# A graph kernel on one core: messages of the later passes in an array of their own, with the two groups of a chunk side by side

## The reference

```python
# layer 0: one pass, weighted
agg = segment_sum(adj_vals[:, None] * xw[edge_src], edge_dst)
# layer 1: messages gated by an MLP of the edge attributes, back to the source
msg = gate * h[dst] * (cw * mj)[:, None]
agg = segment_sum(msg, src);  tot = segment_sum(mj, src)
# layer 2: two weighted passes
x = segment_sum(x[src] * edge_weight[:, None], dst)
# layer 3 (Chebyshev, K = 4): three unweighted passes
prop = segment_sum(w[:, None] * h[row], col)
```

## Time and profile before

| | |
|---|---|
| time of three runs | 16256.79 us median, 16254.69 to 16295.25 |
| the profiled execution's own time | 16257.53 us, for a span of 16255.7 us |
| busy: PE, DVE, ACT, POOL | 10843.7, 12042.7, 7461.2, 7855.1 us |
| DMA queues: SP's, POOL's | 3065.78 MB, 57.2% of the 16 engines; 1034.11 MB, 16.5% |
| HBM read, written | 2932.16 MB, 1702.21 MB |

### The profile page before, as it was taken

How to read it: one execution, slowest core, us unless ns; L and a number is a source line. 1 busy time by engine, 2 the same in 40 slices (tenths; PEclk the granted TensorE clock), 3 DMA queues, 4 the chain that set the end, 5 groups by cost and what they waited for, 6 DMA issues and landing times. The chain is left out here.

```text
span 16255.7 us, 582040 instructions
## 1 busy us (share of the span) xinstructions
PE 10843.7 (67%) x194032; PEld 8861.6 (55%) x194033; DVE 12042.7 (74%) x25807; ACT 7461.2 (46%) x21291; POOL 7855.1 (48%) x7665
## 2 busy tenths in 40 slices
PE   5676666666610488867776677777776686676678
PEld 4555555555500366644555556666655565565556
DVE  9666666666633378789996788789778778777776
ACT  0121212121122267744445656766664475475466
POOL 0677777777777366013331067037307605713730
PEclk8777777777755599988888888999997797798789
DMA  8343333333467499879998798889779898988987
GB/s 339 111 124 124 123 123 123 123 123 123 123 170 179 114 364 350 291 257 341 331 309 246 241 337 324 280 307 353 274 261 375 319 313 332 373 277 309 384 289 238
DMA packets 1719990, 4103.19 MB, mean 252 GB/s; under 512 B 337506, under 2 KB 626240, under 8 KB 1719094
## 3 DMA queue, kind: packets, MB, share of 16 engines
q1 hardware_dynamic: 1288470, 3065.78, 57.2%
q0 software_dynamic: 431248, 1034.11, 16.5%
q10 hardware_dynamic: 144, 1.60, 0.0%
HBM read 2932.16 MB, written 1702.21 MB: 285 GB/s over the span
## 5 line engine op out<-in xcount | busy, mean ns | idle before, releaser
L1443 POOL DMA_INDIRECT messages<-exp_stage,exp_block_rows x3324 | 3555.9, 1070 | 4461.9 <-ACT exp_stage L1423 1830.6
L845 POOL DMA_INDIRECT records<-rec,row_i x3125 | 3113.0, 996 | 1444.6 <-issue 814.5
L1584 PEld LDWEIGHTS sum_sums<-sum_slots,sum_onehot 128*128 128x128 bf16 x93072 | 2521.5, 96 | 1135.8 <-issue 1133.7
L1584 PE MATMUL sum_sums<-sum_slots,sum_onehot 128*128 128x48 bf16 (+1 forms) x93072 | 2677.8, 183 | 625.6 <-DVE h L1510 485.3
L1541 ACT ACTIVATE sum_onehot<-iota_b,sum_late_places 128x128 bf16<-128x128 bf16 x5817 | 1910.1, 391 | 765.1 <-PE sum_sums L1584 681.0
L1301 PE MATMUL exp_rows<-tab,h 128*128 x39888 | 1811.7, 197 | 512.7 <-DVE h L1342 225.2
L1307 PE MATMUL exp_rows<-tab,h 128*128 x13296 | 1428.4, 282 | 932.1 <-ACT exp_stage L1423 688.0
L1301 PEld LDWEIGHTS exp_rows<-tab,h 128*128 128x128 bf16 x39888 | 1567.7, 102 | 872.5 <-issue 726.5
L1307 PEld LDWEIGHTS exp_rows<-tab,h 128*128 128x128 bf16 x13296 | 1208.5, 125 | 1151.8 <-issue 1118.9
L668 ACT COPY rec<-emeta 128x40 f32 (+1 forms) x625 | 140.2, 224 | 3064.3 <-DMA records<-rec,row_i 3064.3
L1342 DVE TENSOR_SCALAR h<-exp_places,pcol 128x2048 bf16<-128x2048 bf16 x1662 | 1298.9, 782 | 164.4 <-DMA exp_places<-src_places 140.7
(11 more groups left out here) (299 smaller groups left out, 22128.4 us busy)
## 6 DMA issues: line engine op xcount, KB each, us to landing
sum_slots<-messages SPq DMA_DIRECT2D x1662, 576.0 KB, 5.3
exp_places<-src_places SPq DMA_DIRECT2D x1662, 512.0 KB
sum_slots<-messages SPq DMA_DIRECT2D x277, 600.0 KB, 5.4
messages<-zeros SPq DMA_DIRECT2D x124, 1149.0 KB
l_places<-dst_places SPq DMA_DIRECT2D x277, 512.0 KB, 6.3
recc<-records SPq DMA_DIRECT2D x277, 448.0 KB, 4.7
l_gate<-records SPq DMA_DIRECT2D x277, 448.0 KB
records<-fill SPq DMA_DIRECT2D x215, 576.0 KB, 12.9
```

Source lines behind the costliest of these rows:

```text
L845: pool.indirect_dma_start(rec_dram, bass.IndirectOffsetOnAxis(ap=row_i[:, g, k:k + 1], axis=0), rec[:, g, k, :], None).then_inc(put[g], 16)
L1443: pool.indirect_dma_start(lines, bass.IndirectOffsetOnAxis(ap=row_d[:, c, g:g + 1], axis=0), stage[:, c, g, :], None, element_offset=0 if ...
L1584: last = pe.matmul(sums[:, c % RS, g, 0:width], onehot[:, c % RS, g * B + k, :], of[:, n * width:(n + 1) * width], start=n == 0, stop=n == ...
```

## The change

The array is split in two. `first_messages` has lines of 832 words: type values and the first pass's terms. `messages` holds nothing but terms, for the way back at rows of 600 words and for the later passes, over the same memory, at rows of 576. In both arrays the two groups of a chunk alternate: block p of the chunk's first group is row 2p of the chunk, block p of the second row 2p + 1. So `idx_d` and `idx` have to be turned into the new numbers, ten more instructions on DVE, and a chunk's load of partition p becomes one run of 4608 bytes (4800 on the way back). In the first pass the two runs of 2304 bytes stay two, 1024 bytes apart. The type loads of the gate stage stay two runs of 1024 bytes. Both arrays are set to zero.

```diff
-    LINE = ceil_div(UROW + ROW1 // 2, 32) * 32
+    LINE = UROW + ROW // 2
+    TERMS = ROW1 // 2
...
-    line_dram = nc.dram_tensor("messages", [NBLK, LINE], F32).ap()
-    terms_dram = line_dram.bitcast(BF16)[:, 2 * UROW:2 * UROW + ROW1]
-    msg_dram, back_dram = terms_dram[:, 0:ROW], terms_dram
+    line_dram = nc.dram_tensor("first_messages", [NBLK, LINE], F32).ap()
+    later_dram = nc.dram_tensor("messages", [NBLK * TERMS], F32).ap()
+    msg_dram = later_dram.bitcast(BF16)[0:NBLK * ROW].rearrange("(n f) -> n f", f=ROW)
+    back_dram = later_dram.bitcast(BF16).rearrange("(n f) -> n f", f=ROW1)
+
+    def in_pairs(rows):
+        return rows.rearrange("(c p g) f -> p c (g f)", p=P, g=CH)
...
+                    def zeros(k, i, first):
+                        if first:
+                            to, _, begin = zeroed[k]
+                            sp.dma_start(to[:, 0:begin], zero_dram[:, 0:begin]).then_inc(s_zero, 16)
+                            sp.dma_start(*pieces(k, 0, 1, R5 - 1)).then_inc(s_zero, 16)
+                        else:
+                            sp.dma_start(*pieces(k, i, 0, R5)).then_inc(s_zero, 16)
+
                     def turn(i, first, last):
                         windows_of(i, first, 1)
-                        if first:
-                            sp.dma_start(zeroed[:, 0:BEGIN], zero_dram[:, 0:BEGIN]).then_inc(s_zero, 16)
-                            sp.dma_start(*pieces(0, 1, 2)).then_inc(s_zero, 16)
-                        else:
-                            sp.dma_start(*pieces(i, 0, 3)).then_inc(s_zero, 16)
+                        zeros(0, i, first)
                         attrs(i, first, 1)
                         if not last:
                             windows_of(i + 1, False, 0)
-                        sp.dma_start(*pieces(i, 3, 2)).then_inc(s_zero, 16)
+                        zeros(1, i, first)
...
+                    dve.wait_ge(s_cp, 4)
+                    for n, rows_of in enumerate((idx_d, idx)):
+                        dve.tensor_scalar(place[:, n, :], rows_of[:, :], P - 1, None, ALU.bitwise_and)
+                        dve.tensor_scalar(odd[:, n, :], rows_of[:, :], P.bit_length() - 1, None,
+                                          ALU.logical_shift_right).then_inc(s_cp, 1)
+                        dve.wait_ge(s_cp, 5 + 3 * n)
+                        dve.tensor_scalar(odd[:, n, :], odd[:, n, :], CH - 1, None, ALU.bitwise_and)
...
-            in_order = of_dram.rearrange("(g p) f -> p g f", p=P)
...
-                                sp.dma_start(slots_in[:, c, :, :],
-                                             in_order[:, bass.ds(i * RG + c * CH, CH), 0:length]
-                                             ).then_inc(g_load[c], 16)
+                                sp.dma_start(slots_in[:, c:c + 1, :, :] if len(in_order.shape) == 4 else
+                                             slots_in[:, c:c + 1, :, :].rearrange("p a g f -> p a (g f)"),
+                                             in_order[:, bass.ds(i * RC + c, 1)]).then_inc(g_load[c], 16)
...
-        collect(msg_dram, drel, win_d, acc, D)
+        collect(first_terms, drel, win_d, acc, D)
...
-            collect(msg_dram, rel, win_d, acc, D)
+            collect(in_pairs(msg_dram), rel, win_d, acc, D)
```

More of the change, by code:

```diff
@@ L575, in gnn_kernel, with pieces @@
             s_zero = sem("s1_first_zeroed")
[L577 to L581, removed]
+            def pieces(k, i, g, many):
+                to, piece, begin = zeroed[k]
+                at = i * (R5 * piece) + ((g - 1) * piece + begin)
+                return (to[:, bass.ds(at, many * piece)].rearrange("p (n f) -> p n f", f=piece),
+                        zero_dram[:, 0:piece].unsqueeze(1).to_broadcast([P, many, piece]))
             def batches(engine, step):
@@ L988, in gnn_kernel @@
             beyond = scoped(s2, "beyond", [P, NG], F32)
+            place = scoped(s2, "place_in_group", [P, 2, NG], I32)
+            odd = scoped(s2, "odd_group", [P, 2, NG], I32)
             srel_f = h1[:, :, :].rearrange("p w f -> p (w f)")[:, 0:NS]
@@ L1012, in _ @@
                         dve.scalar_tensor_tensor(out=idx_d[:, :], in0=sent_in[:, :, 2 * B], scalar=-1.0,
-                                                 in1=beyond[:, :], op0=ALU.add, op1=ALU.add)
+                                                 in1=beyond[:, :], op0=ALU.add, op1=ALU.add).then_inc(s_cp, 1)
+                    dve.wait_ge(s_cp, 4)
[5 more added lines that the diff above has]
+                        dve.tensor_scalar(odd[:, n, :], odd[:, n, :], CH - 1, None, ALU.bitwise_and)
+                        with nc.allow_low_precision(reason="block numbers: whole, below 2^24"):
+                            dve.tensor_tensor(place[:, n, :], place[:, n, :], rows_of[:, :], ALU.add).then_inc(s_cp, 1)
+                            dve.wait_ge(s_cp, 6 + 3 * n)
+                            dve.scalar_tensor_tensor(out=rows_of[:, :], in0=odd[:, n, :], scalar=float(1 - P),
+                                                     in1=place[:, n, :], op0=ALU.mult, op1=ALU.add).then_inc(s_cp, 1)
+                            dve.wait_ge(s_cp, 7 + 3 * n)
                 @block.tensor
@@ L1457, in gnn_kernel, with collect @@
         n_sum = [0]
-        def collect(of_dram, rel, row, acc, width):
+        def collect(in_order, rel, row, acc, width):
             length = B * 3 * width
@@ L1867, in _ @@
                             dve.tensor_copy(srel[:, :, :, :], sent_in[:, :, 0:B].unsqueeze(3).to_broadcast([P, NG, B, 2]))
[L1868 removed]
+                collect(in_pairs(back_dram), srel, win_s, acc, MSG)
             square = scoped(s5, "square1", [P, W, D], F32)
```

29 lines of the change are left out of this document (15 added, 14 removed).

## The result

Measured together on one chip, ten runs of each: the changed kernel 16309.44 us (16265.52 to 16355.75), the kernel before 16267.15 us (16242.95 to 16315.93). The ratio is 1.0025, 95% interval 1.0013 to 1.0036. That is within 0.3% and inside the range that was given, but the interval leaves out 1: the forecast was no change at all, and 42 us came.

The account below looks back on a forecast made before the run. Bounds by stage: POOL in edges and unweighted expands, DVE in weighted expands and gate stage, DVE with PE in collects. Sum: 16257.5 + 0 + 0 + 0 + 0 = 16257 us, no change; range 16170 to 16320.

Parts of the forecast that it names:

- The loads: Six later collects: longer runs save 0.27 us a chunk on the DMA engines, 0 on the path; 449 us if uncovered.
- the circle of DVE and PE: Collects: DVE and PE wait on each other, pacing a chunk at 1.90 us and hiding loads of 1.74 us.
- the price of 2.95 us per MB: Collects: cost of short-run loads on 16 engines, 482.2 us for 163.25 MB, giving 1.74 us a chunk.
- The 2.50 us per MB of the store: Store at the start with 4608-byte runs: 75.4 us for 30.19 MB, used to price one-run loads at 1.47 us a chunk.
- SP's wait as a proof: Collects: SP waited 296.9 of 480 us for PE to free buffers; late loads would leave it nothing to wait for.
- The fills: Edges: 161 MB more zeroing costs 0 on the path, covered by POOL's pace; 525 us if uncovered.
- Ten more instructions: Places block: DVE renumbering takes at most 11.3 us, hidden while DVE is idle, so 0 on the path.
- modes of 14 us: Collects: the later one took 14 us more than the first for the same PE count, perhaps quicker beside less traffic.
- The pitch: Scatters: rows at other pitches, unpriced by the trace, taken as 0 on the path.
- Loads bound the collects: Rival, collects: loads set the pace, so the change gains 449 us; chance 0.04 whole, 0.09 a part over 49 us.
- The gate stage waits for landings: Rival, gate stage: scatters landing later delay ACT and then DVE, 269 us slower if scatter time doubles; chance 0.07.
- The fills starve POOL: Rival, edges: fills delay other loads until POOL runs dry, up to 525 us slower; chance 0.02.

Follow-up runs that it names:

- e11_before_bare: Kernel before with collects cut to nearly only their two-run loads (one group's sums, one bfloat16 term, fewer one-hots): 17808.09 us.
- e2_before_more_zero: Kernel before plus 161 MB more zero fills in the edges stage, into an array nothing reads: ratio 1.0005 to the kernel before.
- e9_before_unused_ten: Kernel before plus the ten renumbering DVE instructions and their waits, result unused, old layout: ratio 1.0024 to the kernel before.
- e5_split_only: Kernel before with the two arrays, their pitches and fills, groups in old order, no renumbering, its small tiles present unused: ratio 1.0010 to the kernel before.
- the thin kernels: Kernel before and changed kernel, both with cheaper collects (second group's sums and third terms left out): 18248.49 and 18272.12 us.
- e10_after_far: Changed kernel plus 31 unused copies of the renumbering on four columns (310 small DVE instructions): ratio 1.0021 to the kernel before.

## Why the prediction was right, and where it was not

**The loads: 0 on the path, right; the price, wrong.** The cover was there, wider than claimed: the circle of DVE and PE takes 1.90 us a chunk and the loads in two runs can go at 1.52 (2529.6 / 6 / 277), not 1.74. For one run the 1.47 was right: measured 1.45. The step that failed is the price of 2.95 us per MB for two runs, taken as DMA share times time in a collect that does not wait for its loads. Where it waits for them the same loads cost 1.52 / 0.590 = 2.58 us per MB, so that product says what the packets were recorded to take, not what the loads need. The 2.50 us per MB of the store comes from the same product, but lay near the truth for one run: 412 GB/s is 2.43. The expected share of about 0.80 for the collect therefore did not come; it was 0.90. With the cover gone the change is worth 118 us, not 449.

**SP's wait as a proof, wrong.** The prediction said that a late load would leave SP nothing to wait for. In `e11_before_bare` PE waits 130.1 us for loads and SP still waits 205.1 of 390 us for PE. So SP's wait for a free buffer tells nothing here about late loads. What tells is the other argument, the time from issue to landing against the time until the chunk is read: 5.2 of 9.7 us in the full collect. In the bare one it is 8.0 us, against at most the six chunks of 9.1 us that the ring holds, less the products that come before the issue.

**The fills: 0, right.** Shown alone by `e2_before_more_zero`. Edges' DMA share was given as 0.52 and came to 0.54 there and 0.58 in the changed kernel. Between the earlier trace rows and the changed kernel, 152.4 MB more cost (0.509 - 0.329) x 3900 = 702 us of 16 engines, 4.6 us per MB where the queue's mean of 3.24 was taken. POOL's gaps stayed at 0.3 us.

**Ten more instructions: this step failed.** It said "Hidden; 0, or 11 us were that cover gone". Their own time was hidden (the stage that holds them lasted 1191.7 us in `e9_before_unused_ten` and 1192.8 in `e11_before_bare`). But they move all of DVE's later loops. In the third batch that cost 45 us in the first weighted expand (1193.4 against 1148.5) and some 13 in the collects, in the first batch 20 and 13. The sum had no term for it: it priced the ten instructions by their own time alone. The prediction had named both kinds of stage as paced by DVE, so they were the ones to look at; but DVE's pace alone does not tell the place, since the second and third weighted expands lost nothing (1091.5 and 1097.2 us against 1091.7 and 1092.7). Its remark that modes of 14 us exist in the collects was the right thread, put down to less traffic and given to the wrong sign. (By the stages' lengths, 515.8 and 527.2, it is 11 us.)

**The number.** 42 us came where none was forecast. The range held them by its width and not by a cause that it named: on that side it reached 63 us from the forecast, 49 of them for what a measurement cannot tell from no change and the rest for the gate stage's landings, which had no part in it. The measured time lies 52 us above the forecast.

**The pitch: 0, right.** `e5_split_only` has the pitches without the alternation: ratio 1.0010 with an interval that holds 1, collects 3695.4 us.

**The rivals.** Loads bound the collects: no, by the thin kernels, which run at 1.58 us a chunk without a wait for a load. The gate stage waits for landings: no, 1472.6 us against 1473.8, ACT's wait 624.6 us of 1400 against 601.5 and DVE's 12.4 against 16.0. That a scatter's time could double was the author's assumption; at 7225 to 8625 of the changed kernel POOL's queue had a share of 0.232, so a scatter took 0.232 x 1400 / 524 = 0.62 us of 16 engines, where it had been 0.61. The fills starve POOL: no.

**What stays open.** That ten more instructions ahead of DVE's loops bring the loss, and the layout does not, is shown by `e9_before_unused_ten`. Their spare tiles are not it, since `e5_split_only` has them. That it goes by position is shown by `e10_after_far`: with 310 more the first expand comes back and the pause in the first collect falls below the old one. In the collects the traces show the loss as a longer pause of DVE at fixed instructions; for the first expand it was not narrowed down so far. Why a pause goes by position no run shows. Instructions brought in by DMA in each turn are excluded for the collects: in every one of them, before, after and in both of these experiments, the instruction queues move nothing between 42 us after its start and 30 us before its end. The end of the program, with its two lengths, was seen and not explained either.

## What to carry to other kernels

A DMA share near 0.9 did not say that the loads were near the bound (1.52 us a chunk, where the pace was 1.90). To find the price, cut the engines' work down until something waits for the loads, and read it there. A change of 0.3% or less needs a control in which the new instructions are present and useless: here the position of the later loops cost 33 to 58 us, against at most 118 that the idea is worth. An edit that speeds a resource which something else hides is worth trying again once nothing hides it: the one run would bring up to 118 us if the collects' circle of DVE and PE fell under 1.45 us a chunk.

## What the runs showed that was not expected

- **Position of code.** Ten DVE instructions ahead of a loop added 0.10 to 0.11 us to three of a turn's six chunks in the last collect and took as much from two others, in the median over its turns, so one such step a turn is left; 320 moved the second collect from 530 to 540 us and the last from 532 to 527.
- **The end.** Over the fourteen profiles the last stage took 97 to 98 us at a granted clock of 0.82 to 0.84 seven times, and 153 to 154 us at 0.50 to 0.52 the other seven, in both kernels. The times of a kernel fall in two heaps, some 53 us apart in the kernel before in the first batch (twenty times at 16240 to 16283 us, nine at 16300 to 16326), and where a kernel's two heaps can be told, its profiled execution with the long end lies in the upper one. With ten runs each that alone can shift a median by more than the change did.
- **Bare collects run at half the clock** (granted 0.50, where the full ones have 0.99 to 1.00) with PE busy 240 of 390 us. PE waits 130.1 us for loads even so, so the loads and not the clock set the pace.
- **Batches differ.** In the third batch edges took 4903 us in place of 4065: in `e9_before_unused_ten` POOL waited for DVE 668.6 us of 3900 in that stage, where it waited 109.1 in the first profile of the kernel before. The loss by the ten instructions in the first expand was 20 us in the first batch, 24 to 27 in the second and 45 in the third, so its size depends on more than the position; on what, was not traced.
